# A Mamba-2 block on one Trainium2 core: the Silu product, the gate weights and the output weights take other places in the engines' orders

## The chip, the cores and the metric

The kernel runs on one core of one Trainium2 chip. The metric is the device time of one execution in microseconds (us); the time of a kernel is the median of its runs.

## The reference

One layer norm feeds a Mamba-2 (SSD) block and a small mixture of LoRA experts; both are added to the input. The shapes are 1 x 1024 tokens x 512 channels, 128 heads of 64 channels (8192 inner channels), 8 groups of state size 128, chunks of 128 tokens. Cut to what matters here:

```
xn   = layernorm(x)
proj = xn @ in_proj_w.T                        # gate 8192 | hBC 10240 | dt 128
hBC  = silu(causal_conv4(proj[hBC]) + conv_b)  # hs 8192 | B 8x128 | C 8x128
dt   = clip(softplus(dt + dt_bias), 0, 100);  A_cum = cumsum(-exp(A_log) * dt) per chunk
Y    = (C B^T * L) (hs dt)  +  C S_prev exp(A_cum)  +  hs * D      # per head; L = exp of decays
S    = decayed S_prev + B^T (hs dt decay)
g    = Y * silu(gate);  g = g * rsqrt(mean(g*g over the group) + eps) * norm_w
out  = x + g @ out_proj_w.T + xn @ base_W.T + lora terms
```

## The kernel before

All matmuls on fp32 data are made of three passes over a high part (rounded to a short mantissa) and a low part (the remainder): high x high, high x low, low x high. So each weight has a high copy, made by ScalarE (GH, OH, AH), and a remainder, made by GpSimd or VectorE (GL, OL, AL).

The 8192 inner channels are cut into 16 stages s of 512 channels (8 heads), and the tokens into 8 chunks c. The main loop runs over 128 slots m = 8s + c, and a 129th that only drains. Five programs (TensorE, ScalarE, VectorE, GpSimd, and SyncE for the transfers) are written out by hand; each engine works strictly in its own order and waits on semaphores. In this text slot m is the pass of that loop with this m, on every engine.

In slot m TensorE does, in this order: the transposes of the next slot's convolved channels (T, and the B and C products BG in even stages); the halves of projection tiles that slot_halves assigns (each 12 matmuls of 512 columns, "A"); Off (not for c = 0) and St (not for c = 7), each 3 matmuls, for the state; Y, 64 small matmuls with the decayed scores EM (L400); O of slot m-1, 12 matmuls with the output weights OH and OL; the gate product GT of slot m+1, 12 matmuls with the gate weights GH and GL (L241 to L243); and the transposes GTr of the gated result yb (L417). The big tiles A always use PSUM banks 0 and 1, so a new tile can begin only when the convolution of the last one has read them. The single banks 5, 6 and 7 go round in turn: the product that comes third after T(m+1) in this turn waits until VectorE has made xch and dxh of it.

A projection tile runs as follows: both halves on TensorE, act_tap on ScalarE (L441, one tap and the bias out of PSUM), three more taps on VectorE (dve_conv, L641), tanh of it in th on ScalarE (act_tanh, L447, in the slot that ends the tile), and at the end the Silu product (th+1)*x on VectorE (dve_silu, L647), one slot later. In the loop there are 74 tiles (7 B, 7 C, 60 of hs), and they end in 74 different slots.

ScalarE in slot m: act_front(m+1), which copies T into hsr (L459) and in even stages copies B and C parts, and then makes the decays of slot m+1 (8 Relu of 128 columns at L475, one Exp of 1024 at L478); the gate weights GH of the next stage if c = 7 (L452, four copies); the tap; SH and DH, the high parts of state and dxh; the square of yb (L605); pl (L610 or L615); tg, tanh of the gate (L618, waits for GT of slot m+1); gTh, high part of GTr (L623); the output weights OH if c = 0 (L627, four); the next tile's AH; tanh of the tile.

VectorE in slot m: xch and dxh of slot m+1 (L661, L665, wait for hsr) and in even stages BL and Gt; the gate product tg (L652); yb = Off x decay (L824, waits for Off); the state S (L834); EM of slot m+1 (L682, waits for the Exp); Y + yb (L846); yb = Y x tg (L849); the Silu product and the convolution; al in odd stages (L861); gTl (L865, waits for gTh); OL if c = 0 (L870, four).

GpSimd in slot m: yb + dhs (L932, waits for L824); GL of the next stage if c = 7 (L884, four); CL, SL, DL, the decay of S, and dhs for slot m+1 (L890 to L903); the group's scale; AL (L879); al + pl (L955). Gate and output weights share one landing tile TS: SyncE loads the output weights (L1055) when GL is done and behind the next tile's weights, and the gate weights (L1045) when OL is done.

Of the kernel before, what the change touches and what calls it, by code (L numbers as in the profile page):

```python
# [6 lines left out]
def mamba_moe_block_kernel(nc, x, wa, wg, wo, wdt, cw, cbias, nw, dtb, alog, dvec, wbase, wrt, wla, wlb,  # L7
# [90 lines left out]
    with ctx:  # L98
# [350 lines left out]
        def act_gate_hi(s):  # L449
            se.wait_ge(ts_in, 16 * (2 + 2 * s))  # L450
            for k in range(4):
                se.activation(GH[:, k, :], TS[:, k, :], ACT.Copy).then_inc(s_gh, 1)  # L452

        def act_front(m):
# [5 lines left out]
            if s % 2 == 0:  # L460
                se.wait_ge(s_bg, ngc(m))
                if s and c != 7:
                    se.wait_ge(s_stp, n7(m - 8))
                if s and c:
                    se.wait_ge(s_off, n0(m - 8))
                se.activation(BH[:, c, :], bank("BG", m)[:, 0:128], ACT.Copy).then_inc(s_bh, 1)
                se.activation(CH[:, tok(c)], Cx[:, tok(c)], ACT.Copy).then_inc(s_ch, 1)
            se.wait_ge(rows_in[m % 2], 16 * (m // 2 + 1))
# [25 lines left out]
        def act_program():  # L494
# [83 lines left out]
            act_front(0)  # L578
            act_state_hi(0)
# [5 lines left out]
            for m in range(M + 1):  # L585
                s, c = divmod(m, 8)
                pm, pc, ps = m - 1, (m - 1) % 8, (m - 1) // 8
                done = [k // 2 for k in slot_halves[m + 1] if k % 2] if m < M else []
                if m + 1 < M:
                    act_front(m + 1)  # L590
                if m < M:
                    if c == 7 and s + 1 < NS:
                        se.wait_ge(s_gt, m + 1)
                        act_gate_hi(s + 1)
                    for i in done:
                        act_tap(i)
# [14 lines left out]
                if m and ps % 2:  # L611
                    n_ = ngc(pm)
                    se.wait_ge(pl_in[pc % 2], 16 * ((n_ + 1) // 2))
                    se.wait_ge(s_rst, n_)
                    se.activation(pl[pc % 2][:, :], pl[pc % 2][:, :], ACT.Copy, scale=rst[:, pc, 1:2]).then_inc(s_plr, 1)  # L615
                if m + 1 < M:
                    se.wait_ge(s_gt, m + 2)
                    se.activation(tg[:, :], bank("GT", m + 1), ACT.Tanh, scale=0.5).then_inc(s_tg, 1)  # L618
                if m < M:
# [4 lines left out]
                    if c == 0:  # L624
                        se.wait_ge(ts_in, 16 * (3 + 2 * s))
                        for j in range(4):
                            se.activation(OH[:, j, :], TS[:, j, :], ACT.Copy, scale=nwt[:, 4 * s + j:4 * s + j + 1]).then_inc(s_oh, 1)  # L627
# [57 lines left out]
        def dve_program():  # L685
# [126 lines left out]
            for m in range(M + 1):  # L812
                s, c = divmod(m, 8)
                pm, pc, ps = m - 1, (m - 1) % 8, (m - 1) // 8
                if m + 1 < M:
                    dve_front(m + 1)
                if m < M:
                    dve_gate(m)
                    o = bank("St", m) if c != 7 else None
# [17 lines left out]
                if m < M:  # L837
# [12 lines left out]
                    for k in slot_halves[m]:  # L850
                        if k % 2:
                            dve_silu(k // 2)
                    for k in slot_halves[m + 1]:
                        if k % 2:
                            dve_conv(k // 2)
# [7 lines left out]
                if m < M:  # L863
                    ve.wait_ge(s_gth, m + 1)
                    ve.tensor_tensor(gTl[:, :, :], bank("GTr", m).rearrange("p (k t) -> p k t", k=4),  # L865
                                     as_f(gTh[:, :, :]), ALU.subtract).then_inc(s_gtl, 1)
                    if c == 0:
                        for j in range(4):
                            ve.wait_ge(s_oh, 4 * s + j + 1)
                            ve.scalar_tensor_tensor(out=OL[:, j, :], in0=TS[:, j, :], scalar=nwt[:, 4 * s + j:4 * s + j + 1],  # L870
                                                    in1=as_f(OH[:, j, :]), op0=ALU.mult, op1=ALU.subtract).then_inc(s_ol, 1)

# [8 lines left out]
        def pool_gate_lo(n):  # L881
            for k in range(4):
# [22 lines left out]
        def pool_program():  # L905
# [20 lines left out]
            for m in range(M + 1):  # L926
                s, c = divmod(m, 8)
                if m < M:
                    if c:
# [3 lines left out]
                    if c == 7 and s + 1 < NS:  # L933
                        pool_gate_lo(2 + s)
# [177 lines left out]
```

## Time and profile before

| | |
|---|---|
| median of 3 runs | 1797.67 us (1797.47 to 1800.89) |
| profiled execution | 1797.44 us, of which the span from first to last instruction is 1796.1 us |
| mean granted TensorE clock | 0.991 of full speed |
| TensorE busy (matmuls) | 1688.6 us, 94% of the span |
| VectorE / ScalarE / GpSimd busy | 77% / 69% / 60% |
| memory traffic | 202.57 MB, mean 113 GB/s |

The profile is of one execution. A row of a timeline has the start, the duration, the engine, the line, the operation and its tiles; in brackets stands how long the engine had been idle before it and what released it. PE is the matmul side of TensorE and PEld its weight loads, which run ahead of the matmuls. The time outside the span is 1.3 us. Two stages, one even and one odd, make a period of about 211 us, and the waits repeat with it.

### The profile page before, as it was taken

The page shows a single profiled execution, that of the slowest core. Times are in us where ns is not written, and L with a number is a line of the kernel's source. Part 1 is how long each engine was busy: PE and PEld are TensorE (multiplying, and loading weights), DVE is VectorE, ACT ScalarE, POOL GpSimd, SP SyncE. Part 2 cuts the span into 40 slices and gives each one's busy share as a digit, 9 for nine tenths or more (in the row PEclk, how much of TensorE's full clock was granted, in tenths as well). Part 3 has the DMA queues.
Part 4 walks back from the last instruction along what each step waited for, and adds up shares of the span by engine and source line. Part 5 has one row for each costly group of instructions (what it writes and reads, how often), then busy time and mean ns, then how long its engine had stood idle before and what let it go on. Part 6 is the DMA issues. An engine that isn't in the chain of part 4 may idle for free.

```text
span 1796.1 us, 32206 instructions
## 1 busy us (share of the span) xinstructions
PE 1688.6 (94%) x11244; PEld 1355.8 (75%) x11244; DVE 1381.9 (77%) x1793; ACT 1246.5 (69%) x2687; POOL 1082.6 (60%) x1037
## 2 busy tenths in 40 slices
PE   6979999999999999999999999999999999999988
PEld 4767777787777877778777777778777787777766
DVE  6768778886887878887778877887687877878765
ACT  5167676776767777676776777777667777677775
POOL 3036467665676656665567556765566755776575
PEclk9989999999999999999999999999999999999999
DMA  3242143332433234332333324342343323433142
GB/s 122 91 148 93 62 145 127 120 108 88 133 124 120 86 101 143 120 124 75 131 120 135 98 78 151 112 142 87 100 133 116 130 76 103 143 124 104 65 141 95
DMA packets 97167, 202.57 MB, mean 113 GB/s; under 512 B 28392, under 2 KB 29936, under 8 KB 92784
## 3 DMA queue, kind: packets, MB, share of 16 engines
q1 hardware_dynamic: 97008, 200.51, 33.6%
q8 instruction: 92, 1.51, 0.3%
q14 instruction: 67, 0.55, 0.1%
HBM read 162.20 MB, written 38.28 MB: 112 GB/s over the span
## 4 chain that ended last, share of the span: by engine, by line
PE 68%; DVE 16%; POOL 6%; ACT 5%; issue 5%; DMA 0%; DVEq 0%; ACTq 0%; SPq 0%; POOLq 0%
PE P L241 20%; PE P L243 19%; PE P L242 18%; DVE hsX L641 5%; PE P L400 5%; POOL GL L884 4%; DVE hsX L647 2%; PE P L287 2%; PE P L417 2%; DVE Bx L641 1%; ACT P L475 1%; DVE P L846 1%; DVE yb L849 1%; DVE EM L682 1%; POOL yb L932 1%
## 5 line engine op out<-in xcount | busy, mean ns | idle before, releaser
L932 POOL TENSOR_TENSOR yb<-yb,dhs 128x512 f32<-128x512 f32 x112 | 144.2, 1287 | 412.0 <-DVE yb L824 412.0
L475 ACT ACTIVATE P<-AB,SC 128x128 f32<-128x128 f32 x1024 | 308.7, 370 | 0.0
L241 PE MATMUL P<-xh,AH 128*128 128x512 f32 x656 | 270.2, 412 | 37.8 <-DVE hsX L641 32.3
L641 DVE SCALAR_TENSOR_TENSOR hsX<-P,cwt,hsX 128x1023 f32<-128x1023 f32 (+2 forms) x192 | 245.5, 1279 | 18.1 <-ACT hsX L441 13.6
L243 PE MATMUL P<-xh,AL 128*128 128x512 f32 x656 | 257.4, 392 | 0.0
L242 PE MATMUL P<-xl,AH 128*128 128x512 f32 x656 | 257.2, 392 | 0.0
L618 ACT ACTIVATE tg<-P 128x512 f32<-128x512 f32 x127 | 76.0, 598 | 255.2 <-PE P L243 255.2
L241 PE MATMUL P<-GH,xh 128*128 128x512 f32 x544 | 220.7, 406 | 16.2 <-POOL GL L884 16.2
L241 PE MATMUL P<-OH,gTh 128*128 128x512 f32 x512 | 213.8, 418 | 2.3 <-issue 2.2
L243 PE MATMUL P<-GH,xl 128*128 128x512 f32 x544 | 214.0, 393 | 0.0
L242 PE MATMUL P<-GL,xh 128*128 128x512 f32 x544 | 213.7, 393 | 0.0
L865 DVE TENSOR_TENSOR gTl<-P,gTh 128x512 fp32r<-128x512 f32 x128 | 88.2, 689 | 162.8 <-ACT gTh L623 162.8
L879 POOL TENSOR_TENSOR AL<-AR,AH 128x512 fp32r<-128x512 f32 x82 | 107.7, 1314 | 161.4 <-ACT AH L429 161.4
L893 POOL TENSOR_TENSOR SL<-S,SH 128x512 fp32r<-128x512 f32 x112 | 148.3, 1324 | 90.4 <-ACT SH L486 88.2
L243 PE MATMUL P<-OH,gTl 128*128 128x512 f32 x512 | 201.3, 393 | 0.0
L242 PE MATMUL P<-OL,gTh 128*128 128x512 f32 x512 | 201.0, 393 | 0.0
L605 ACT ACTIVATE sq<-yb 128x512 bf16<-128x512 f32 x128 | 80.7, 630 | 138.5 <-DVE yb L849 138.0
L241 PEld LDWEIGHTS P<-xh,AH 128*128 128x128 f32 x656 | 124.3, 189 | 68.3 <-DVE hsX L641 37.9
L682 DVE TENSOR_TENSOR EM<-P,Gt 128x1024 f32<-128x1024 f32 x128 | 155.9, 1218 | 24.4 <-issue 16.6
L400 PEld LDWEIGHTS P<-xch,EM 128*64 128x64 f32 x4096 | 129.9, 138 | 50.5 <-issue 42.5
L896 POOL TENSOR_TENSOR DL<-dxh,DH 128x512 fp32r<-128x512 f32 x112 | 153.0, 1366 | 3.3 <-ACT DH L492 3.3
L400 PE MATMUL P<-xch,EM 128*64 128x64 f32 x4096 | 147.5, 225 | 4.7 <-DVE xch L661 2.9
(181 smaller groups left out, 4067.7 us busy)
## 6 DMA issues: line engine op xcount, KB each, us to landing
AB<-acr_d SPq DMA_DIRECT2D x128, 512.0 KB, 4.9
AR<-in_wa SPq DMA_DIRECT2D x80, 256.0 KB, 2.8
TS<-in_wg SPq DMA_DIRECT2D x16, 1024.0 KB, 5.0
TS<-in_wo SPq DMA_DIRECT2D x16, 1024.0 KB, 5.4
part_d<-pl SPq DMA_DIRECT2D x64, 256.0 KB, 3.2
pl<-part_d SPq DMA_DIRECT2D x64, 256.0 KB, 2.7
al<-acc_d SPq DMA_DIRECT2D x64, 256.0 KB, 3.0
acc_d<-al SPq DMA_DIRECT2D x58, 256.0 KB, 2.2
```

Source lines behind the costliest of these rows:

```text
L241: te.matmul(o, ah_, bh_, start=(first and i == 0), stop=False)
L242: te.matmul(o, ah_, bl_, start=False, stop=False)
L243: r = te.matmul(o, al_, bh_, start=False, stop=(last and i == n - 1))
L400: r = te.matmul(o[f:f + 64, h * 64:(h + 1) * 64], EM[m % 2][:, at_ + f:at_ + f + 64], xch[m % 2][:, h * 64:(h + 1) * 64], start=True, stop ...
L475: r = se.activation(E[:, h, :], AB[m % 2][:, h, :], ACT.Relu, bias=SC[s % 2][:, c, 3, h:h + 1], scale=-1.0)
L641: ve.scalar_tensor_tensor(out=o[:, d:T], in0=raw[:, 0:T - d], scalar=cwt[:, n, 3 - d:4 - d], in1=o[:, d:T], op0=ALU.mult, op1=ALU.add).the ...
L682: ve.tensor_tensor(EM[m % 2][:, :].rearrange("p (h l) -> p h l", h=8), E[:, :, :], Gt[:, c, :].unsqueeze(1).broadcast_to([128, 8, 128]), A ...
L865: ve.tensor_tensor(gTl[:, :, :], bank("GTr", m).rearrange("p (k t) -> p k t", k=4), as_f(gTh[:, :, :]), ALU.subtract).then_inc(s_gtl, 1)
L879: pe_.tensor_tensor(AL[i % 2][:, :, :], AR[i % 2][:, :, :], as_f(AH[i % 2][:, :, :]), ALU.subtract).then_inc(ring_lo, 1)
L893: pe_.tensor_tensor(SL[:, :], S[:, :], as_f(SH[:, :]), ALU.subtract).then_inc(s_sl, 1)
L896: pe_.tensor_tensor(DL[:, :], dxh[:, :], as_f(DH[:, :]), ALU.subtract).then_inc(s_dl, 1)
L932: pe_.tensor_tensor(yb[:, :], yb[:, :], dhs[:, :], ALU.add).then_inc(s_tp, 1)
```

## The change

Four moves; no operation is added or removed, and no size changes.

1. VectorE: in slots that end a tile and come directly after a slot that ended one, the Silu product of the earlier tile stands ahead of the off-diagonal scaling (L824). In other slots it stays behind L849.
2. ScalarE: in slots with c = 7 the four gate-weight copies no longer follow the decays as one block: two stand between the copy of T and the decays, two behind the decays. GpSimd makes the first two remainders ahead of its sum yb + dhs and the other two behind it.
3. ScalarE: in slots with c = 0 the four output-weight copies stand ahead of the gate's tanh (L618), instead of behind gTh. They now wait there for the product O of the slot before, which is the last to read the old ones.
4. VectorE: in slots with c = 0 the four output-weight remainders stand ahead of gTl.

```diff
-        def act_gate_hi(s):
+        def act_gate_hi(s, ks=range(4)):
...
+        def act_decay(m):
+            s, c = divmod(m, 8)
             se.wait_ge(rows_in[m % 2], 16 * (m // 2 + 1))
...
+                new_gate = c == 7 and s + 1 < NS
                 if m + 1 < M:
                     act_front(m + 1)
+                    if new_gate:
+                        se.wait_ge(s_gt, m + 1)
+                        act_gate_hi(s + 1, (0, 1))
+                    act_decay(m + 1)
+                    if new_gate:
+                        act_gate_hi(s + 1, (2, 3))
                 if m < M:
-                    if c == 7 and s + 1 < NS:
-                        se.wait_ge(s_gt, m + 1)
-                        act_gate_hi(s + 1)
                     for i in done:
                         act_tap(i)
...
+                if m < M and c == 0:
+                    se.wait_ge(ts_in, 16 * (3 + 2 * s))
+                    if m:
+                        se.wait_ge(s_o, m)
+                    for j in range(4):
+                        se.activation(OH[:, j, :], TS[:, j, :], ACT.Copy, scale=nwt[:, 4 * s + j:4 * s + j + 1]).then_inc(s_oh, 1)
                 if m + 1 < M:
                     se.wait_ge(s_gt, m + 2)
                     se.activation(tg[:, :], bank("GT", m + 1), ACT.Tanh, scale=0.5).then_inc(s_tg, 1)
...
-                    if c == 0:
-                        se.wait_ge(ts_in, 16 * (3 + 2 * s))
-                        for j in range(4):
-                            se.activation(OH[:, j, :], TS[:, j, :], ACT.Copy, scale=nwt[:, 4 * s + j:4 * s + j + 1]).then_inc(s_oh, 1)
...
+                new_tiles = [k // 2 for k in slot_halves[m + 1] if k % 2] if m < M else []
                 if m < M:
                     dve_gate(m)
+                    if new_tiles:
+                        for k in slot_halves[m]:
+                            if k % 2:
+                                dve_silu(k // 2)
                     o = bank("St", m) if c != 7 else None
...
-                    for k in slot_halves[m]:
-                        if k % 2:
-                            dve_silu(k // 2)
-                    for k in slot_halves[m + 1]:
-                        if k % 2:
-                            dve_conv(k // 2)
+                    if not new_tiles:
+                        for k in slot_halves[m]:
+                            if k % 2:
+                                dve_silu(k // 2)
+                    for i in new_tiles:
+                        dve_conv(i)
...
                 if m < M:
-                    ve.wait_ge(s_gth, m + 1)
-                    ve.tensor_tensor(gTl[:, :, :], bank("GTr", m).rearrange("p (k t) -> p k t", k=4),
-                                     as_f(gTh[:, :, :]), ALU.subtract).then_inc(s_gtl, 1)
                     if c == 0:
                         for j in range(4):
                             ve.wait_ge(s_oh, 4 * s + j + 1)
                             ve.scalar_tensor_tensor(out=OL[:, j, :], in0=TS[:, j, :], scalar=nwt[:, 4 * s + j:4 * s + j + 1],
                                                     in1=as_f(OH[:, j, :]), op0=ALU.mult, op1=ALU.subtract).then_inc(s_ol, 1)
+                    ve.wait_ge(s_gth, m + 1)
+                    ve.tensor_tensor(gTl[:, :, :], bank("GTr", m).rearrange("p (k t) -> p k t", k=4),
+                                     as_f(gTh[:, :, :]), ALU.subtract).then_inc(s_gtl, 1)
...
-        def pool_gate_lo(n):
-            for k in range(4):
+        def pool_gate_lo(n, ks=range(4)):
+            for k in ks:
...
                 if m < M:
+                    if c == 7 and s + 1 < NS:
+                        pool_gate_lo(2 + s, (0, 1))
                     if c:
                         pe_.wait_ge(s_t1, n0(m))
                         pe_.wait_ge(s_dhs, m + 1)
                         pe_.tensor_tensor(yb[:, :], yb[:, :], dhs[:, :], ALU.add).then_inc(s_tp, 1)
                     if c == 7 and s + 1 < NS:
-                        pool_gate_lo(2 + s)
+                        pool_gate_lo(2 + s, (2, 3))
```

## Rows read from the trace of the kernel before

**Rows 1.** The page, part 1: busy time of each engine.
```profile
...
PE 1688.6 (94%) x11244; PEld 1355.8 (75%) x11244; DVE 1381.9 (77%) x1793; ACT 1246.5 (69%) x2687; POOL 1082.6 (60%) x1037
```

**Rows 2.** Waits of weight loads: line, releaser, total us, times, longest.
```profile
...
PEld P L241 <- DVE hsX L641: 37.9, 24, 2.2
PEld P L241 <- POOL GL L884: 34.2, 45, 1.7
PEld P L241 <- DVE xch L661: 18.2, 9, 2.4
...
PEld P L241 <- DVE Bx L641: 5.7, 7, 0.8
```

**Rows 3.** The same view for the matmuls.
```profile
...
PE P L241 <- POOL GL L884: 16.2, 32, 1.2
```

**Rows 4.** Timeline, weight loads, slot 59: start, us, instruction, idle before, releaser.
```profile
...
913.29 0.19 PEld L241 LDWEIGHTS P<-xh,AH 128*128 128x128 f32 x1 [1.59 <-DVE hsX L641]
```

**Rows 5.** Timeline of VectorE in slot 58.
```profile
...
903.67 0.69 DVE L824 TENSOR_TENSOR yb<-P,SC 128x512 f32<-128x512 f32 x1 [3.01 <-PE P L243]
...
907.42 1.99 DVE L647 SCALAR_TENSOR_TENSOR hsX<-th,hsX 128x1024 f32<-128x1024 f32 x1
909.33 3.91 DVE L641 SCALAR_TENSOR_TENSOR hsX<-P,cwt,hsX 128x1023 f32<-128x1023 f32 x3
```

**Rows 6.** Timeline of VectorE, a Silu product of slot 54.
```profile
...
849.82 1.22 DVE L647 SCALAR_TENSOR_TENSOR hsX<-th,hsX 128x1024 f32<-128x1024 f32 x1
```

**Rows 7.** Waits of weight loads in slots 55, 47, and from 1695 on.
```profile
...
PEld P L241 <- POOL GL L884: 2.8, 3, 1.7
...
PEld P L241 <- POOL GL L884: 1.8, 3, 0.7
...
PEld P L241 <- POOL GL L884: 2.1, 3, 0.7
```

**Rows 8.** Timeline of ScalarE in slot 55.
```profile
...
858.86 1.01 ACT L478 ACTIVATE P<-P 128x1024 f32<-128x1024 f32 x1
```

**Rows 9.** Timeline of GpSimd in slot 47.
```profile
...
758.32 5.05 POOL L884 TENSOR_TENSOR GL<-TS,GH 128x512 fp32r<-128x512 f32 x4
```

**Rows 10.** Timeline, weight loads, slot 55's last gate weights.
```profile
...
866.75 0.19 PEld L241 LDWEIGHTS P<-GH,xh 128*128 128x128 f32 x1 [0.71 <-POOL GL L884]
```

**Rows 11.** Windows: us, busy by engine, PEclk, DMA share, GB/s.
```profile
...
867.00:871.00 4.00, 4.00 (x16) 3.38 (x16) 1.24 (x2) 2.37 (x6) 1.94 (x2) 0.57 0.86 246
```

**Rows 12.** Timeline of ScalarE in slot 47.
```profile
...
755.91 1.01 ACT L478 ACTIVATE P<-P 128x1024 f32<-128x1024 f32 x1
756.83 2.18 ACT L452 ACTIVATE GH<-TS 128x512 fp32r<-128x512 f32 x4
```

**Rows 13.** Timeline of VectorE in slot 47.
```profile
...
757.01 1.23 DVE L682 TENSOR_TENSOR EM<-P,Gt 128x1024 f32<-128x1024 f32 x1
...
760.14 3.92 DVE L641 SCALAR_TENSOR_TENSOR hsX<-P,cwt,hsX 128x1023 f32<-128x1023 f32 x3 [0.26 <-ACT hsX L441]
```

**Rows 14.** Timeline, weight loads, slot 48's first tile half.
```profile
...
765.32 0.19 PEld L241 LDWEIGHTS P<-xh,AH 128*128 128x128 f32 x1
```

**Rows 15.** Timeline, weight loads, slot 49.
```profile
...
782.39 0.19 PEld L241 LDWEIGHTS P<-DH,BH 128*128 128x128 f32 x1 [2.39 <-DVE xch L661]
```

**Rows 16.** Timeline of ScalarE in slots 48 and 49.
```profile
...
774.47 0.71 ACT L615 ACTIVATE pl<-pl,rst 128x512 f32<-128x512 f32 x1
...
776.79 2.56 ACT L627 ACTIVATE OH<-TS,nwt 128x512 fp32r<-128x512 f32 x4
```

**Rows 17.** Timeline of VectorE in slot 49.
```profile
...
777.55 3.57 DVE L870 SCALAR_TENSOR_TENSOR OL<-TS,nwt,OH 128x512 fp32r<-128x512 f32 x4
```

**Rows 18.** Timeline of VectorE in slot 57, two output-weight remainders.
```profile
...
882.16 1.41 DVE L870 SCALAR_TENSOR_TENSOR OL<-TS,nwt,OH 128x512 fp32r<-128x512 f32 x2
```

**Rows 19.** Timeline of the DMA queue in slot 48.
```profile
...
768.77 0.43 SPq L1055 DMA_DIRECT2D TS<-in_wo  x1
```

**Rows 20.** The line L1055: its 15 loads of output weights, time to landing.
```profile
...
DMA to landing us min/median/max: 4.7/5.4/6.0
```

More of the change, by code:

```diff
@@ L578, in act_program @@
             act_front(0)
+            act_decay(0)
             act_state_hi(0)
@@ L879, in pool_ring @@
             pe_.tensor_tensor(AL[i % 2][:, :, :], AR[i % 2][:, :, :], as_f(AH[i % 2][:, :, :]), ALU.subtract).then_inc(ring_lo, 1)
-        def pool_gate_lo(n):
-            for k in range(4):
+        def pool_gate_lo(n, ks=range(4)):
+            for k in ks:
                 pe_.wait_ge(s_gh, 4 * n + k + 1)
```

## The prediction

> **What bounds the kernel now.** I read the page first: TensorE's matmuls are busy for 1688.6 of 1796.1 us, the other engines for 60 to 77% [rows 1]. So only time in which TensorE stands still can be won, and the next view is the waits of its weight loads, where nearly all of that time has four names [rows 2]: the first half of a new tile waits for the convolution of the last one (37.9 us for hs tiles, 5.7 for B tiles), the gate product for the remainders GL (34.2), and the state product St, in slots with c = 1, for xch and dxh (18.2). The view of the matmuls puts the GL waits at 16.2 us [rows 3]: a load runs ahead of its matmul, so the load's idle time is above the true loss and the matmul's is below it. Where one long wait stands alone the two agree; where three short ones follow each other, as before GL, I take 80% of the load's figure, nearer to it because a modelled matmul end lies later than the true one.
>
> The pattern repeats every two stages. I followed one period (slots 47 to 62) through the timeline of each engine, and price each wait there.
>
> **Part 1, the Silu product.** In slot 58 VectorE finishes the gate product, then stands idle 3.01 us until TensorE delivers Off, and only then works through L824 to L849. Behind L849 come the Silu product (1.99 us) and the three taps (3.91 us) [rows 5]. The next slot's tile wants those banks and waits 1.59 us, until 913.29 [rows 4]. The change puts the Silu product into the idle stretch: the taps then begin at 907.42 instead of 909.33, 1.9 us earlier, which is more than the wait. The tanh that it needs was made a slot before. What hides it is that idle time: 3.01 us here, 2 to 3 us in the other places (slots with c = 2, 5 and 6); in odd slots with c = 1 VectorE has none, but part 4 takes the output-weight remainders out of them. The product also gets shorter there: alone it took 1.22 us [rows 6], beside GpSimd's DL and S 1.99.
>
> By slot_halves the move acts in 29 slots, and the next slots hold just the waits of rows 2, except two of the hs waits at the start, the longest (2.2 us) and a short one (0.2): 37.9 - 2.4 + 5.7 = 41.1 us, rounded. In B slots the tap on ScalarE ends as L849 does, so only about 1.1 us can be won there, still more than their 0.82. **Part 1: 41.1 us**; bounds 0 (if something else holds the taps) and 41.1.
>
> **Part 2, the gate weights.** Each of the 15 stage changes has three waits on GL: 2.8 us where an even stage ends, 1.8 where an odd one does, 2.1 at the last [rows 7]; at 80% that is 2.3, 1.4 and 1.7. The change starts two of the four copies 3.4 us earlier (8 Relu and an Exp lie between), and GpSimd, idle then, makes two remainders ahead of its sum. The other two keep their time on ScalarE, but two fewer stand ahead of them on GpSimd, so they are done some 2.5 us earlier (four took 5.05 [rows 9]).
>
> The price: the Exp ends later by two copies, 2.18 / 2 = 1.09 us [rows 12], and with it EM, L846, L849 and what follows.
>
> - Even stages (slot 55): the Exp ended at 859.87 [rows 8], so the last two copies now end near 862.05 and the last remainder near 864.1. TensorE, 0.8 us earlier by part 1, would want it near 866.75 - 2.3 - 0.8 = 863.6 [rows 10]. A wait of some 0.5 stays; 1.8 us won, seven times: 12.6 us. At the last change about 1.2.
> - The waits also cost clock. In 867 to 871 the granted clock is 0.57, that is, TensorE runs at its 1.2 GHz level for most of this stretch, right behind the three waits [rows 11]; two stretches like it, at 443 (0.61) and 1290 (0.57), stand behind the same waits of other stages. Half speed there costs (1 - 0.57) x 4 = 1.7 us, with the others 5.0 us. With the waits gone I take all of it back: bounds 0 and 5.0.
> - Odd stages (slot 47): here a tile ends too, and the taps start at 760.14, held by EM's chain and by the tap on ScalarE. EM began at 757.01, right behind the Exp [rows 12, 13]. It now begins near 758.1, L849 ends near 760.5, the taps (3.92 us) near 764.45. TensorE wants the banks at 765.32 [rows 14] less the 1.4 that GL no longer takes: 763.9. So a new wait of 0.55 us appears: 0.8 won, seven times: 5.6 us.
>
> **Part 2: 12.6 + 1.2 + 5.0 + 5.6 = 24.4 us**; bounds 10 (the Exp's delay lands in full, 15 x 1.09 = 16 us off the 27 that GL can give, and the clock stays as it is) and 32.
>
> **Parts 3 and 4, the output weights.** In even stages St of slot 49 waits 2.39 us for dxh [rows 15]; 7 such waits make 16.7 of the 18.2. dxh is late because ScalarE copies OH (2.56 us) ahead of hsr [rows 16] and VectorE makes OL (3.57 us) ahead of xch [rows 17]. The change puts OH behind L615, at 775.2 (that work ended at 775.18), where ScalarE waited for GT anyway. Now OH ends near 777.7, tg and gTh follow 1.8 us later than before, and hsr near 779.3, 0.5 us earlier than before. VectorE starts OL near 775.7 and not at 777.55, and has gTl behind it instead of ahead: 1.85 - 0.65 = 1.2 us earlier for xch and dxh. **7 x 1.2 = 8.4 us.** The bounds are 0.5 and 2.2 us a time, from OL's duration: beside nothing two took 1.41 [rows 18], so four take 2.8; beside GpSimd's sum they took 3.57. I take 3.57, since the new place lies beside dhs and al + pl.
>
> The Trainium skill (GPSIMD Engine Reference, Specifications) says that GpSimd shares its SBUF interfaces with VectorE and that they contend where a VectorE instruction has two SBUF inputs, as OL has. By that rule OL keeps the long duration and the gain is 1.2 us a time; with OL as in rows 18 it would be about 2.0 and the whole part 14 us.
>
> In odd stages, at c = 0, VectorE and ScalarE have more idle time than OL and OH take (they wait for gTh and for GT there), so both are hidden; nothing waited for them on TensorE, but slot 57 becomes light enough for its Silu product. At the very end (slot 121) OH ahead of tanh brings nothing: St there waits for gTl, which gets later, and Y for dxh, which doesn't move. I take 0.
>
> **The sum.** 41.1 + 24.4 + 8.4 = 73.9 us. From the profiled execution's 1797.44 us that leaves 1723.5; the median of the runs lies 0.2 above that execution, so **1724 us**.
>
> **The rivals.**
>
> 1. All waits vanish, no new one appears: 41.1 + 27.4 (80% of GL) + 5.0 + 7 x 2.2 = 89 us, 1708 us. For it: slack of 1 to 3 us in most slots. Against: the two chains of part 2 come out too long by half a microsecond on rows of this trace. 13%.
> 2. The taps don't start earlier, since the tap on ScalarE or EM's chain holds them in these slots too: part 1 is 0, the time 1765 us. For it: in slots 47 and 54 the tap ends just as the taps can start. Against: in slot 58 they started right behind the Silu product, without idle time. 8%. A mixture, part 1 won in half of its slots (each has only 0.2 to 0.4 us to spare), gives 1745: 14%.
> 3. Slower: the output-weight copies now stand ahead of tg, gTh and hsr, and wait there for their transfer. Its issue in slot 48 is at 768.77, behind a tile's weights [rows 19], and transfers took up to 6.0 us [rows 20]: landed at 774.8, and the copy's new place opens at 775.2. Every microsecond of lateness would go into tg, gTh, hsr and St, 16 times. To eat 74 us it would have to be 4.6 us late in every stage; 0.4 us of slack, and GL and AL that now come earlier and let the issue go at about 767, speak against. It would give 1800 us or more. 3%.
> 4. No change within what this measurement can tell (0.2%, 3.6 us): the waits reappear elsewhere one for one, because VectorE is the true bound. Against: 77% busy, and it idles for 3.01 us right ahead of L824 [rows 5]. 2%.
>
> The forecast itself (1712 to 1736) has 60%. **Range 1706 to 1750**: it takes in rival 1 and the mixture, and leaves out rivals 2 to 4. Faster by over 0.2% 0.94, within 0.03, slower 0.03.
>
> **What the profile after would show.** Part 1: Silu products (L647) of about 1.2 us ahead of L824 in 29 places, and the waits on hsX and Bx down to the 2.4 us of the start plus 7 new ones near 0.5 us in slots after odd c = 7. Part 2: waits on GL under 5 us in total, GL split around L932, no stretch at half clock at 443, 867 and 1290. Parts 3 and 4: St's waits for xch at c = 1 near 1.2 us, OL still about 3.6 us for four in even stages. Wrong would be: taps that wait for L441; TensorE waiting on yb at L417 in slots with c = 7, if the Exp's delay goes further than the taps; or ScalarE waiting for a DMA ahead of OH.

## The result and the profile after

| | before | after |
|---|---|---|
| median of 4 runs each | 1798.90 us | 1740.38 us (1738.93 to 1742.34) |
| span of the profiled execution | 1796.1 us | 1740.0 us |
| mean granted TensorE clock | 0.991 | 0.992 |

The changed kernel takes 0.967 of the time (95% interval 0.9657 to 0.9683): 58.5 us less, where 74 were forecast. The time lies inside the range and 16 us above the forecast. Lines have shifted: tap product and convolution are now L651, the Silu product L657, xch L671, yb L839, Exp and EM L481 and L692, al L876, OL L882, gTl L885, GL L899.

The page after, busy times (against [rows 1]: TensorE lost 12.5 us of busy time and 56 us of span):

```profile
PE 1676.1 (96%) x11244; PEld 1354.9 (78%) x11244; DVE 1377.6 (79%) x1793; ACT 1243.3 (71%) x2687; POOL 1069.6 (61%) x1037
```

The waits of weight loads after (total, times, longest), the answer to [rows 2]:

```profile
PEld P L241 <- DVE gTl L885: 14.4, 15, 3.5
PEld P L292 <- DVE al L876: 10.5, 7, 1.5
...
PEld P L241 <- POOL GL L899: 7.7, 16, 0.9
PEld P L241 <- DVE Cx L651: 7.7, 7, 1.1
PEld P L241 <- DVE xch L671: 5.7, 8, 0.9
PEld P L241 <- DVE hsX L651: 3.9, 9, 2.2
```

The old names have shrunk: hsX from 37.9 to 3.9, GL from 34.2 to 7.7, xch from 18.2 to 5.7, and Bx is gone. Three new names stand there: the B products BG (L292) wait seven times 1.5 us for al, a tile half seven times 1.1 us for the taps of a C tile, and Off waits for gTl.

Slot 58 of VectorE after, the answer to [rows 5]:

```profile
872.88 1.22 DVE L657 SCALAR_TENSOR_TENSOR hsX<-th,hsX 128x1024 f32<-128x1024 f32 x1
875.28 0.69 DVE L839 TENSOR_TENSOR yb<-P,SC 128x512 f32<-128x512 f32 x1 [1.18 <-PE P L243]
...
879.03 3.91 DVE L651 SCALAR_TENSOR_TENSOR hsX<-P,cwt,hsX 128x1023 f32<-128x1023 f32 x3
```

The Silu product lies in the idle stretch and takes 1.22 us, not 1.99; 1.18 us of idle time are left and the taps follow the gate product at once.

**Where the time came from.** The length of slot m is measured here from TensorE's first load of L417 in slot m-1 to its first one in slot m. In each trace the seven periods repeat to a few hundredths, but for stretches at half clock and for late transfers of the output weights (see below), which are left out.

| us per period | before | after | forecast gain | gain |
|---|---|---|---|---|
| slots 55 to 58 (even stage ends, odd one starts) | 55.95 | 52.97 | 4.2 | 3.0 |
| slots 43 and 46 (hs tiles alone) | 26.75 | 23.44 | 3.3 | 3.3 |
| slots 47 to 49 (odd stage ends, even one starts) | 38.49 | 37.49 | 2.0 | 1.0 |

The shortfall is 1.2 x 7 in the first group and 1.0 x 7 in the third, 15.4 us, and slot 121 takes 1.1 us more than before (13.77 against 12.69): together about the 16 us that are missing. The three stretches at half clock of [rows 11] are gone, as forecast; slot 121 has a new one, which is looked at below. The experiments ask what took the place of each.

### The profile page after: what moved, and what is told of

Its sections match the earlier page's. It is cut to its first block, busy times and chain, and to the rows that moved or that the text cites. A ratio compares the mean times of both kernels' runs of the same rounds, so it can differ in the third digit from the quotient of the medians.

```text
span 1740.0 us, 32221 instructions
## 1 busy us (share of the span) xinstructions
PE 1676.1 (96%) x11244; PEld 1354.9 (78%) x11244; DVE 1377.6 (79%) x1793; ACT 1243.3 (71%) x2687; POOL 1069.6 (61%) x1037
## 4 chain that ended last, share of the span: by engine, by line
PE 74%; DVE 9%; ACT 8%; issue 6%; POOL 3%; DMA 1%; DVEq 0%; ACTq 0%; SPq 0%; POOLq 0%
PE P L241 22%; PE P L243 20%; PE P L242 20%; PE P L400 6%; ACT P L478 3%; PE P L287 2%; PE P L417 2%; DVE Cx L651 2%; DVE OL L882 1%; DVE hsX L651 1%; ACT GH L452 1%; POOL DL L911 1%; DVE P L861 1%; DVE hsX L657 1%; POOL GL L899 1%
## 5 line engine op out<-in xcount | busy, mean ns | idle before, releaser
L651 DVE SCALAR_TENSOR_TENSOR hsX<-P,cwt,hsX 128x1023 f32<-128x1023 f32 (+2 forms) x192 | 245.6, 1279 | 16.3 <-ACT hsX L441 11.8
L241 PE MATMUL P<-GH,xh 128*128 128x512 f32 x544 | 216.9, 399 | 2.7 <-POOL GL L899 2.7
L692 DVE TENSOR_TENSOR EM<-P,Gt 128x1024 f32<-128x1024 f32 x128 | 156.1, 1220 | 46.5 <-issue 31.3
L885 DVE TENSOR_TENSOR gTl<-P,gTh 128x512 fp32r<-128x512 f32 x128 | 88.2, 689 | 115.4 <-ACT gTh L637 115.4
L671 DVE TENSOR_TENSOR xch<-P,SC 128x512 f32<-128x512 f32 x128 | 88.1, 688 | 87.8 <-ACT hsr L459 87.7
```

What stands on the lines that cost most here:

```text
L241: te.matmul(o, ah_, bh_, start=(first and i == 0), stop=False)
L651: ve.scalar_tensor_tensor(out=o[:, d:T], in0=raw[:, 0:T - d], scalar=cwt[:, n, 3 - d:4 - d], in1=o[:, d:T], op0=ALU.mult, op1=ALU.add).the ...
L692: ve.tensor_tensor(EM[m % 2][:, :].rearrange("p (h l) -> p h l", h=8), E[:, :, :], Gt[:, c, :].unsqueeze(1).broadcast_to([128, 8, 128]), A ...
```

## Experiments

Each was timed against the kernel before on its own chip, whose median there was 1799.0 to 1800.4 us; ratios compare best.

**The parts alone and taken out.** Part 1 alone, put on the kernel before:

```diff
                     dve_gate(m)
+                    if new_tiles:
+                        for k in slot_halves[m]:
+                            if k % 2:
+                                dve_silu(k // 2)
```

> Kernel before with part 1 alone (the Silu product ahead of L824 in 29 slots). Theory A, the prediction's: the 29 waits on the convolution vanish by themselves, 41 us won, about 1758 us. Rival B, the parts help each other: in odd slots with c = 1 VectorE is only light enough once the output-weight remainders are gone, so there (7 slots) nothing is won, and about 30 us remain, 1769 us. In its profile, A wants waits of the new tile on hsX near 3 us in total and on Bx at 0; B wants 7 hsX waits of about 1.6 us left.

Measured: 1771.61 us, 0.9844 (0.9826 to 0.9862), 28.8 us won, not 41. Slots 43 and 46 gave the forecast in full (23.44). Slots 55 to 58 gave 0.95 instead of 2.4: slot 55 only 0.33, because most of the rest of the 0.82 us of the Bx wait went into the waits for GL, whose time GpSimd sets. By the loads they total 36.1 us, against 34.2 [rows 2]; by the matmuls 18.2, against 16.2 [rows 3]:

```profile
PEld P L241 <- POOL GL L895: 36.1, 45, 1.7
```

And slots 57 and 58 gave 0.7 of 1.6. Neither theory fits: the waits on hsX total 6.0 us in this trace, where A wanted near 3 and B seven times 1.6 more. Behind the now longer GL waits a stretch at half clock stood at four of the seven even stage ends (before: at three of seven, [rows 11]), and two more stood in slots like 49. The stage end at slot 39, weight loads and then the window (columns as in [rows 11]):

```profile
643.65 0.19 PEld L241 LDWEIGHTS P<-GH,xh 128*128 128x128 f32 x1 [0.66 <-POOL GL L895]
...
647.00:651.00 4.00, 3.91 (x14) 3.39 (x15) 0.85 (x2) 1.98 (x4) 2.27 (x3) 0.57 0.69 195
```

Part 2 alone (GpSimd's remainders are split in the same way, cut here and in the later splits):

```diff
                     act_front(m + 1)
+                    if new_gate:
+                        se.wait_ge(s_gt, m + 1)
+                        act_gate_hi(s + 1, (0, 1))
+                    act_decay(m + 1)
+                    if new_gate:
+                        act_gate_hi(s + 1, (2, 3))
```

> Kernel before with part 2 alone (gate weights split around the decays). Theory A: each stage end is won by what the prediction said, 24 us in all, about 1774 us. Theory C, from the trace of the changed kernel: the won time comes back one or two slots later, as a wait of BG for al behind odd stages (1.5 us, 7 times) and of the first tile half for the convolution of a C tile behind even ones (1.1 us, 7 times), so that about 11 us are won, 1787 us. The half-clock stretches at the ends of stages 2, 4 and 12 are gone in both.

Measured: 1772.42 us, 0.9852 (0.9835 to 0.9868), 28.0 us won. Slots 47 to 49 take 37.75 instead of 38.49 us, 0.74 won where 0.8 was forecast, and slots 55 to 58 take 53.64 instead of 55.95, 2.3 won where 1.8 was. Both new waits are there already, BG's for al (10.5 us) and the C tile's (5.7 us), but theory C took too much off for them. No stretch at half clock stands at a stage end (those of the kernel before stood at the ends of stages 2, 6 and 10, not 2, 4 and 12).

Parts 3 and 4 alone (part 3's lines shown):

```diff
+                if m < M and c == 0:
...
+                        se.activation(OH[:, j, :], TS[:, j, :], ACT.Copy, scale=nwt[:, 4 * s + j:4 * s + j + 1]).then_inc(s_oh, 1)
                 if m + 1 < M:
                     se.wait_ge(s_gt, m + 2)
```

> Kernel before with parts 3 and 4 alone (output weights ahead of the gate's tanh, their remainders ahead of gTl). Theory A: 1.2 us in each of 7 even stages, 8 us, about 1790 us. Theory C, from the trace of the changed kernel: 1.1 us seven times, less 1.1 us in slot 121, where St waits for gTl: 6.6 us, about 1792 us. Rival: ScalarE waits for the transfer of the output weights, each microsecond of it lands in St, and the kernel is not faster.

Measured: 1799.06 us, 0.9996 (0.9986 to 1.0005): nothing. VectorE in slot 65, with parts 3 and 4 alone and then before:

```profile
987.72 4.70 DVE L875 SCALAR_TENSOR_TENSOR OL<-TS,nwt,OH 128x512 fp32r<-128x512 f32 x4
...
992.94 0.67 DVE L669 TENSOR_TENSOR xch<-P,SC 128x512 f32<-128x512 f32 x1
...
989.93 3.55 DVE L870 SCALAR_TENSOR_TENSOR OL<-TS,nwt,OH 128x512 fp32r<-128x512 f32 x4
993.40 0.68 DVE L661 TENSOR_TENSOR xch<-P,SC 128x512 f32<-128x512 f32 x1
```

The slot begins at 987.13 with the change and at 987.77 before. So OL starts 1.57 us earlier in it (0.59 against 2.16 us after the slot's begin), but takes 1.15 us longer and has gTl (0.6) behind it: xch starts 0.2 us later than before (5.81 against 5.63), and slots 47 to 49 take 38.65 us instead of 38.49.

The other way round, each part taken out of the changed kernel (the same lines put back as they were), first part 2:

> The changed kernel with part 2 undone (parts 1, 3 and 4 left). If the parts add up as the prediction had them, part 2 is worth 24 us here and this kernel takes about 1764 us. If part 2's gain comes back as the two new waits, it is worth about 11 us and this kernel takes about 1751 us. If part 2 is worth nothing, it equals the changed kernel, 1740 us. The waits of BG for al (10.5 us) and on the C tile's convolution (7.7 us) should both be absent.

Measured: 1770.24 us, 0.9836 (0.9819 to 0.9852); part 2 is worth 29.9 us on top of the others. Both new waits, BG's for al and the C tile's, are absent, so it is part 2 that brings them. Slots 47 to 49 took 38.67 us, but 40.12 in four of seven periods, where a stretch at half clock stood behind two waits (weight loads, then the window):

```profile
1392.13 0.19 PEld L241 LDWEIGHTS P<-SH,CH 128*128 128x128 f32 x1 [2.02 <-DVE gTl L883]
...
1393.34 0.19 PEld L241 LDWEIGHTS P<-DH,BH 128*128 128x128 f32 x1 [0.68 <-DVE xch L669]
...
1394.00:1398.00 4.00, 4.00 (x39) 3.06 (x39) 3.87 (x6) 1.83 (x3) 3.06 (x4) 0.63 0.79 322
```

Part 1 taken out:

> The changed kernel with part 1 undone (parts 2 to 4 left). Part 1 alone was worth 28.5 us on the kernel before. If the parts help each other (with GL no longer making TensorE wait behind the B tile, and the output-weight remainders out of the slots with c = 1), it is worth more here, about 32 us, and this kernel takes 1772 us. If it is worth the 28.5 us here too, 1769 us; if the prediction's 41.1 us, 1781 us.

Measured: 1774.64 us, 0.9863 (0.9848 to 0.9878); part 1 is worth 34.3 us on top of the others.

Parts 3 and 4 taken out:

> The changed kernel with parts 3 and 4 undone (parts 1 and 2 left). Parts 3 and 4 alone moved the kernel before by less than 1 us. By the traces so far their worth lies in slots 41 and 42 and their like, where VectorE must be rid of the remainders for the Silu product to fit: 0.7 us seven times, and 0.3 us in slots like 49. So this kernel should take 5 to 7 us more than the changed one, 1746 us. If the parts are independent, it equals the changed one, 1741.

Measured: 1740.80 us, 0.9676 (0.9661 to 0.9691); they are worth 0.4 us, less than this measurement can tell from nothing. Slots 47 to 49 go from 37.75 to 37.49 by them, a gain of 0.26 a period, 1.8 in all. With part 2 in and these parts out, OL ends clear of GpSimd's work and takes 2.74 us in its old place, and St waits only 1.56 us, not 2.39:

```profile
754.24 2.74 DVE L883 SCALAR_TENSOR_TENSOR OL<-TS,nwt,OH 128x512 fp32r<-128x512 f32 x4
```

So part 2 had already won much of what parts 3 and 4 were to win, and the new place put OL back beside GpSimd (4.71 us, below).

Slot 121 takes 12.70 us without these parts and 13.77 with them, but their order does not decide it. In either order the slot holds one wait of 3.3 to 3.5 us. It takes 12.7 us in the four traces in which no stretch at half clock stands in it (before, part 1 alone, parts 3 and 4 taken out, and the kernel of "Where the C tile's wait comes from", which has the new order), and 13.8 to 15.2 in the ten in which one does, two of them in the old order. The weight load and the window in that kernel with the new order:

```profile
1659.00 0.19 PEld L241 LDWEIGHTS P<-DH,BH 128*128 128x128 f32 x1 [3.43 <-DVE gTl L890]
...
1658.00:1662.00 4.00, 2.72 (x38) 2.04 (x39) 4.00 (x8) 3.75 (x11) 0.67 (x2) 1.00 0.49 143
```

**Where BG's wait comes from.** The single bank that BG(48) wants is that of O(47), and al, its reader, stands behind the convolution on VectorE. In the changed kernel, VectorE and then the weight load:

```profile
735.33 1.23 DVE L692 TENSOR_TENSOR EM<-P,Gt 128x1024 f32<-128x1024 f32 x1 [1.06 <-ACT P L481]
...
737.81 3.91 DVE L651 SCALAR_TENSOR_TENSOR hsX<-P,cwt,hsX 128x1023 f32<-128x1023 f32 x3
741.63 0.74 DVE L876 SCALAR_TENSOR_TENSOR al<-P,rst,al 128x512 f32<-128x512 f32 x1
...
742.42 0.14 PEld L292 LDWEIGHTS P<-ident,Bx 128*128 128x128 f32 x1 [1.50 <-DVE al L876]
```

If the order is at fault, al ahead of the taps ends it; if it is the sum of VectorE's work, the tile will wait instead:

```diff
+                    if ps % 2 and c == 7:
+                        dve_al(m)
                     for i in new_tiles:
                         dve_conv(i)
-                if m and ps % 2:
+                if m and ps % 2 and c != 7:
+                    dve_al(m)
```

> The changed kernel, but in slots with c = 7 of odd stages al (of slot m-1) stands ahead of the convolution instead of behind it. Theory: the 1.5 us that BG waits in slot 48 is the bank that al must free, and al only stands behind 3.9 us of taps. Then that wait (10.5 us in 7 places) is gone from the waits, but the taps end 0.7 us later and the first tile half now waits for them by about 0.9 us: 3 to 4 us won, ratio to the kernel before 0.965. Rival, the prediction's own: it is the convolution that is late; then BG's place shows a wait as long as before or longer, now on the taps, and nothing is won.

Measured: 1740.78 us, 0.9677 (0.9664 to 0.9690), no gain. BG's wait is gone, and the tile half right behind BG waits 1.11 us in its place; slots 47 to 49 take 37.87 us:

```profile
742.89 0.19 PEld L241 LDWEIGHTS P<-xh,AH 128*128 128x128 f32 x1 [1.11 <-DVE hsX L651]
```

So what is late is the chain Exp, EM, taps plus al, in whatever order its last two stand. One gate-weight copy ahead of the Exp instead of two, in odd stages, starts that chain 0.55 us earlier:

```diff
-                        act_gate_hi(s + 1, (0, 1))
+                        act_gate_hi(s + 1, (0,) if s % 2 else (0, 1))
                     act_decay(m + 1)
                     if new_gate:
-                        act_gate_hi(s + 1, (2, 3))
+                        act_gate_hi(s + 1, (1, 2, 3) if s % 2 else (2, 3))
```

> The changed kernel, but in odd stages one gate-weight copy (and remainder) stands ahead of the decays and three behind, instead of two and two. Theory: each copy ahead delays the Exp by 0.55 us, and with it EM, L864, the taps and al; so BG's wait in slot 48 falls from 1.5 to about 1.0 us, and a wait of at most 0.3 us on GL appears in slot 47: 1 to 3 us won. Rival: the tap on ScalarE holds the taps there (it ends at 737.40, L864 at 737.89), then at most 0.4 us of the 0.55 arrives and the two effects cancel: no change.

Measured: 1737.46 us, 0.9660 (0.9647 to 0.9673). BG's wait falls to 1.0, slots 47 to 49 only from 37.49 to 37.40: most of what slot 48 wins (12.86 to 12.35), slots 47 and 49 lose. The medians differ by 2.9 us, but the intervals (0.9647 to 0.9673 here, 0.9657 to 0.9683 for the changed kernel) overlap, and 0.1 a period is 0.6 us. Of the 4.3 us between the two profiled spans 1.8 lie ahead of the loop's first L417 and 1.6 behind its last, which the edit does not touch, and 0.5 are a late transfer in one period of the changed kernel. So this edit is not shown to win more than the 0.6 us.

**Where the C tile's wait comes from.** In slot 56 ScalarE's hsr waits for GpSimd's dhs, which stands behind DL; DL takes 2.27 us beside a Silu product. Without part 2 GpSimd is still at GL then, and DL comes when the Silu product is over: it took 1.28 us there (slot 55 of the kernel without part 2) and hsr waited 0.20 us. GpSimd, ScalarE, VectorE and the weight load in turn:

```profile
840.25 2.27 POOL L911 TENSOR_TENSOR DL<-dxh,DH 128x512 fp32r<-128x512 f32 x1
842.48 1.05 POOL L918 TENSOR_TENSOR dhs<-hsr,Dbc 128x512 f32<-128x512 f32 x1
...
843.62 0.60 ACT L459 ACTIVATE hsr<-P 128x512 f32<-128x512 f32 x1 [1.19 <-POOL dhs L918]
...
850.12 3.91 DVE L651 SCALAR_TENSOR_TENSOR Cx<-P,cwt,Cx 128x1023 f32<-128x1023 f32 x3
...
854.08 0.19 PEld L241 LDWEIGHTS P<-xh,AH 128*128 128x128 f32 x1 [1.10 <-DVE Cx L651]
```

If that is the cause, the B tile's Silu product taken out of DL's way, to ahead of EM in even slots with c = 7, ends it:

```diff
+                early = m < M and c == 7 and not new_tiles
+                if early:
+                    for k in slot_halves[m]:
+                        if k % 2:
+                            dve_silu(k // 2)
                 if m + 1 < M:
                     dve_decay(m + 1)
...
-                    if not new_tiles:
+                    if not new_tiles and not early:
```

> The changed kernel, and the Silu product of the B tile in slots with c = 7 of even stages stands ahead of EM, where VectorE idles 1.9 us for the Exp. Theory: in slot 56 hsr waits 1.2 us for GpSimd's dhs, which is late because DL, beside the Silu product, took 2.27 us instead of 1.28; everything up to the C tile's taps is late by that, and TensorE waits 1.1 us for them in slot 57. Then DL takes 1.3 us, hsr starts 1.0 us earlier and that wait falls to about 0.1 us in 7 places: 7 us won, ratio to the kernel before 0.963. Rival: the Exp's delay by the gate copies alone makes the taps late; then the wait stays near 1.1 us and nothing is won.

Measured: 1735.91 us, 0.9644 (0.9631 to 0.9657), 4.5 us less than the changed kernel. GpSimd and ScalarE there:

```profile
834.34 2.27 POOL L954 TENSOR_TENSOR yb<-yb,dhs 128x512 f32<-128x512 f32 x1
...
839.07 1.28 POOL L916 TENSOR_TENSOR DL<-dxh,DH 128x512 fp32r<-128x512 f32 x1
...
841.44 0.60 ACT L459 ACTIVATE hsr<-P 128x512 f32<-128x512 f32 x1 [0.20 <-POOL dhs L923]
```

DL is back at 1.28 us, hsr waits 0.20 instead of 1.19, and the wait on Cx is gone: slot 57 lost 1.0 us. The price is in the first row: the sum now lies beside the Silu product and takes 2.27 us, GL comes later (waits 10.0 instead of 7.7 us) and slot 55 takes 0.34 more.

**Where the output weights' gain went.** VectorE in slot 49 of the changed kernel, and TensorE's loads:

```profile
752.09 4.71 DVE L882 SCALAR_TENSOR_TENSOR OL<-TS,nwt,OH 128x512 fp32r<-128x512 f32 x4
...
757.92 0.68 DVE L675 TENSOR_TENSOR dxh<-P,SC 128x512 f32<-128x512 f32 x1
...
757.45 0.19 PEld L241 LDWEIGHTS P<-SH,CH 128*128 128x128 f32 x1 [0.75 <-DVE gTl L885]
...
758.66 0.19 PEld L241 LDWEIGHTS P<-DH,BH 128*128 128x128 f32 x1 [0.68 <-DVE xch L671]
```

OL takes 4.71 us, not 3.57 [rows 17], and all of it still stands ahead of gTl, xch and dxh. Two of the four, put behind the gate product of the next slot, should shorten this chain by their share:

```diff
                     dve_gate(m)
+                    if c == 1 and s % 2 == 0:
+                        for j in (2, 3):
+                            ve.wait_ge(s_oh, 4 * s + j + 1)
...
-                        for j in range(4):
+                        for j in range(2 if s % 2 == 0 else 4):
```

> The changed kernel, but in even stages only two of the four output-weight remainders OL stand ahead of gTl in the slot with c = 0; the other two follow the gate product of the next slot. Theory: slot 49 waits 0.75 us for gTl and 0.68 us for xch because four OL took 4.7 us there, beside GpSimd's dhs and al + pl, instead of the 2.8 us that four take alone. With two fewer in the way both waits go, about 1.4 us in 7 places, and the two moved ones take 0.7 us each, since GpSimd is idle there; 8 to 10 us won, ratio to the kernel before 0.962. Rival: ScalarE, which makes hsr only behind OH, tg and gTh, holds xch too; then at most 0.5 us a place is won, 3 us.

Measured: 1733.32 us, 0.9632 (0.9619 to 0.9645), 7 us less than the changed kernel; slot 49 falls from 13.22 to 12.08 us.

```profile
750.70 2.34 DVE L887 SCALAR_TENSOR_TENSOR OL<-TS,nwt,OH 128x512 fp32r<-128x512 f32 x2
...
755.95 1.41 DVE L833 SCALAR_TENSOR_TENSOR OL<-TS,nwt,OH 128x512 fp32r<-128x512 f32 x2
```

The two that stay take 2.34 us beside GpSimd's S, dhs and al + pl, the two that moved 1.41, as in [rows 18].

**All of it together.** The two edits that won, the split of one and three, and the old order of the output weights in the last stage only:

```diff
-                if m < M and c == 0:
+                if m < M and c == 0 and s < NS - 1:
...
+                    if c == 0 and s == NS - 1:
+                        se.wait_ge(ts_in, 16 * (3 + 2 * s))
```

> The changed kernel with four mends together: the B tile's Silu product ahead of EM in slots with c = 7; one gate-weight copy ahead and three behind the decays in odd stages; two output-weight remainders of even stages in the next slot; and in the last stage the order of before for the output weights. If the mends act each at its own place, 4.7 + 2 + 9 + 1 us come off: about 1724 us, ratio 0.958. If the places are links of one chain, in which VectorE is the true bound from slot 48 to 50, the third and second give little and it stays near 1733.

Measured: **1728.29 us (1726.65 to 1731.02), 0.9612 (0.9599 to 0.9625)**, faster than both kernels, and 4 us short of the 1724 expected. Slots 55 to 58 take 52.28 us and slots 47 to 49 36.38; with the split of OL alone these took 36.33, so the split of one and three added nothing there. The old order brought nothing in slot 121 either: its wait of 3.35 us came back, a stretch at half clock stood there, and the slot took 14.2 us (13.77 in the changed kernel, which has a stretch too).

```profile
1651.10 1.35 PEld L400 LDWEIGHTS P<-xch,EM 128*64 128x64 f32 x32 [3.35 <-DVE xch L675]
...
1647.00:1655.00 8.00, 4.83 (x41) 3.79 (x42) 7.97 (x13) 6.83 (x16) 3.86 (x5) 0.80 0.41 139
```

The last run put all four gate-weight copies behind the decays in odd stages, with the two winning moves of VectorE kept, to see whether one VectorE chain sets slots 47 to 49:

```diff
-                        act_gate_hi(s + 1, (0, 1))
+                        act_gate_hi(s + 1, () if s % 2 else (0, 1))
                     act_decay(m + 1)
                     if new_gate:
-                        act_gate_hi(s + 1, (2, 3))
+                        act_gate_hi(s + 1, range(4) if s % 2 else (2, 3))
```

> Two of the four mends of the last combination (the B tile's Silu product ahead of EM, two output-weight remainders in the next slot), with the last stage as in the changed kernel, and in odd stages no gate-weight copy ahead of the decays: all four behind them, as before the change. The prediction gave part 2 in odd stages 0.8 us a place, 5.6 us in all; by that this kernel is 5 to 6 us slower than the last combination, 1734 us. If slots 47 to 49 are one chain that VectorE sets, the 1.4 us that TensorE then waits for GL in slot 47 is time it would have waited for al in slot 48 anyway, the three slots together stay within 0.3 us of 36.4, and the kernel takes 1727 to 1729 us. If the longer wait lets the clock fall, stretches of 1.5 us come on top in some periods.

Measured: 1736.54 us, 0.9652 (0.9639 to 0.9665). Slots 47 to 49 take 37.59 us, 1.2 more than with one copy ahead; three waits on GL (1.8 us) and one on yb (1.0 us) are back in them:

```profile
PEld P L241 <- POOL GL L909: 1.8, 3, 0.7
...
PEld P L241 <- DVE yb L844: 1.0, 1, 1.0
```

My theory of one chain falls. With no copy ahead slots 47 to 49 take 37.59 us, with one 36.38 and with two 36.33: part 2 is worth 1.26 us a period in odd stages here, and 1.18 with OL in the way (38.67 against 37.49). The expectation's price of 0.8 gave 1734.

## Why the prediction was right or wrong

The range held, but partly by luck: part 1 was priced too high and parts 3 and 4 far too high, and part 2 too low. Alone, part 1, part 2 and parts 3 and 4 give 28.8, 28.0 and 1.3 us, 58.1 together, about the measured 58.5.

**Part 1: the mechanism holds, the size was off.** 41.1 us forecast, 28.8 alone, 34.3 on top of the others. The step that failed is the addition of all waits on hsX and Bx as if each would be won. The hs tiles of slots 43 and 46 gave 3.31 a period, all of it. Bx's 0.82 gave 0.33: the next wait, GL's, stands on GpSimd and took the rest, and the forecast itself said that TensorE would want GL "0.8 us earlier by part 1" but did not charge for it where part 2 leaves a wait. Of slot 58's 1.6 us, slots 57 and 58 gave 0.7 without part 4 and 1.38 with it.

**Part 2: the sum is right, by errors that cancel.** 24.4 us forecast, 29.9 on top of the others, 28.0 alone. By slots: taking it out costs 1.41 in slots 55 to 58 and 1.18 in slots 47 to 49, 2.6 x 7 = 18.1 us against a forecast of (1.8 + 0.8) x 7 = 18.2. The match is luck: slot 55 gave 2.4 where 1.8 was forecast, and slot 57 lost 1.0. The last stage change gave 1.5 (forecast 1.2). The six stretches at half clock at stage ends and in slots like 49 cost 8.3 us without part 2, two of 1.24 and four of 1.45, where 5.0 had been taken from the kernel before. About 2 us of the 29.9 lie ahead of the loop, which the edit does not touch.

The step that missed slot 57's loss is the price of part 2: it followed the Exp's delay down VectorE, but not what the earlier remainders do on GpSimd. DL now comes earlier, beside a Silu product that stays behind L849 and has moved later with the Exp; DL stretches, and through dhs, hsr, the Exp and EM the taps of the C tile come 1.1 us late (7.7 us in all). Taking the product away from DL removed the wait, which shows the cause. In odd stages the forecast put the new wait at the tile half and at 0.55 us; it came earlier, at BG, and at 1.5 us. The step that missed it is the list of what stands behind the taps: al was not in it, and BG needs the bank that al reads. The slot after returned most of that time, since it had been waiting for VectorE anyway (against the kernel without part 2, slot 48 +1.48, slot 49 -1.29).

**Parts 3 and 4: wrong.** 8.4 us forecast, 0.4 measured on top of the others and 1.3 alone. Two steps failed. OL was priced at 3.57 us for its new place and took 4.70 and 4.71, outside the 2.8 and 3.57 that the rows gave; alone, with the start 1.57 and not 1.85 us earlier, that is the whole gain (1.57 - 1.15 - 0.6 = -0.2). And the forecast took the 2.39 us of St's wait as it was before, though part 2 left only 1.56 of it, with OL at 2.74 us. The wait for xch did fall from 2.4 to 0.7, as forecast or better, but 0.75 of it stands one product earlier, as a wait for gTl. By the difference of the runs, slots 47 to 49 gained 0.26 of 1.2. Moving half of OL out won 7 us, which shows that this chain set the time. Slot 121 was taken at 0, and 0 is what the traces without a stretch at half clock show (12.7 us in either order). In the changed kernel a stretch stands there, behind St's wait for gTl:

```profile
1663.61 0.19 PEld L241 LDWEIGHTS P<-DH,BH 128*128 128x128 f32 x1 [3.47 <-DVE gTl L885]
...
1662.00:1666.00 4.00, 2.38 (x23) 1.69 (x25) 4.00 (x8) 3.97 (x12) 0.70 (x1) 0.74 0.40 131
```

The forecast asked for GL waits under 5 us and got 7.7, and for OL near 3.6.

**The rivals.** The first (everything vanishes, 1708) and the last (no change) are out. The mixture, 1745, is nearest in time, but for another reason: the moves worked where they were made, and new waits stood elsewhere. The second (taps that don't start earlier, 1765) is out too: in slots 43 and 46 the whole wait went. The late transfer of the third did show, in one place of the changed kernel's trace, and with it one of the forecast's own signs of being wrong: ScalarE waited 1.83 us for the output weights ahead of OH.

```profile
1159.64 2.56 ACT L629 ACTIVATE OH<-TS,nwt 128x512 fp32r<-128x512 f32 x4 [1.83 <-DMA TS<-in_wo]
```

It cost 0.5 us there (slots 79 to 81 took 37.96 us). In the kernel with OL split, where the chain is shorter, a wait of 1.69 us cost all of 1.7 (slots 15 to 17: 38.05 against 36.33). Such waits stand in four of the nine other traces that have part 3's order, in at most two places each, and in none of the four without it. They are rare and short, so the kernel is not slower for them, but the margin of 0.4 us was as thin as the forecast feared. Of the last the kernel has something: in slot 48 VectorE's chain sets the time, and another order of it brought nothing.

**Open.** Which of several equal places gets a stretch at half clock was not settled, nor whether the order of the output weights makes one in slot 121 more likely. Why the transfer of the output weights is late in some places and not in others was not tried.

## What to carry to other kernels

When a wait is removed, ask for every instruction that stands behind the moved work on the same engine, and for every bank or buffer that it frees: here al, right behind the taps, made the new wait, and DL, which came earlier, ran into a Silu product. A wait is worth its length only if the next one is not set by another engine; add up waits of one slot by engine, not by name. Long two-input work on VectorE is best placed where GpSimd has nothing that others wait for, since both stretch; and a chain gets shorter by work taken out of it, not by its start alone.

## What the runs showed of the hardware

**Beside each other VectorE and GpSimd both run slower, more than I had priced.** In one kernel and another the same instruction took: DL 1.28 and 2.27 us, the sum yb + dhs 1.29 and 2.27, the longer time each time beside a Silu product; the Silu product 1.22 and 1.99; two OL 1.41 and 2.34. GpSimd's S took 1.06 in slot 56 and 2.06 beside OL:

```profile
750.38 2.06 POOL L914 TENSOR_TENSOR S<-S,EA 128x512 f32<-128x512 f32 x1
```

The Trainium skill (GPSIMD Engine Reference, Key points) says that GpSimd shares its SBUF interfaces with VectorE and contends with VectorE instructions that have two SBUF inputs; this trace agrees, and adds sizes: 1.6 to 1.9 times the short duration in the pairs above, on either side, and less where the two overlap less (the Silu product took between 1.5 and 2.0 us in most of its places before). Beside the taps, which read one operand from PSUM, DL kept its 1.29 us (slot 56).

**Stretches at half clock stood behind short waits.** With part 1 alone, three waits on GL of 0.7 to 1.7 us were followed by a window at 0.57 (1.2 GHz for most of it), and the same slots in other periods with the same waits by none. A stretch cost 1.2 us (55.6 against 54.38, without part 2) to 1.7 (57.6 against 55.95, before), but whether it comes can't be read from the waits alone: at even stage ends three in seven places before and four in seven with part 1 alone. Between slot 2 and slot 120 the four traces without part 2 have three, three, six and six stretches, and the ten with it none, though one of them (no copy ahead of the decays in odd stages) kept three waits on GL of up to 0.7 us at the odd stage ends.
